# The second half of the residual moved ahead of the masked maxima in the last step of an attention tile

## The reference, cut to what matters

```
x = L0_attn_x                                   # 16 x 2048 x 1024, float32
# layernorm, attention with a window of 128, 16 heads of 64, residual
x = x + _L0_attn_ref(_layernorm(x), w_qkv, w_out)
# layernorm, then two linear layers with ternary weights and 8-bit activations,
# gelu between them, residual
x = x + _L0_ffn_ref(_layernorm(x), W1, b1, W2, b2)

allowed = (j <= i) & (j > i - WINDOW)
scores = jnp.where(allowed, scores, -jnp.inf)
attn = jax.nn.softmax(scores, axis=-1)
```

## Time and profile before

| what | us |
|---|---|
| median of 3 runs | 1665.79 |
| lowest and highest of these | 1577.72, 1676.39 |
| the profiled execution, device time | 1573.67 |
| its span on the slowest core (core 2) | 1571.9 |
| its spans on the eight cores | 1557.0 to 1571.9 |

### The profile page before, as it was taken

One profiled execution on the slowest core, in us unless ns is written; L12 is line 12 of the kernel. 1 busy time (PEld: TensorE's weight loads), 2 busy tenths in 40 slices (PEclk: granted clock), 3 DMA queues, 4 the chain that ended last, 5 costly groups with the idle time before them and its releaser, 6 DMA issues.

```text
span 1571.9 us, 33942 instructions; the slowest of 8 cores (1557.0 to 1571.9 us)
## 1 busy us (share of the span) xinstructions
PE 1489.5 (95%) x11685; PEld 838.6 (53%) x11748; DVE 1072.7 (68%) x2697; ACT 797.8 (51%) x1836; POOL 250.2 (16%) x199
## 2 busy tenths in 40 slices
PE   3789999999899999989999999999999999999998
PEld 3556677667566676644444444444444444444443
DVE  2468888888788999776666666666566666656653
ACT  3667877777677777754333333333333333333321
POOL 0000012222223333103010101101010110101000
PEclk9799999999999999999999999999999999999999
DMA  9768878677776676444424334343443424334332
GB/s 296 212 157 230 236 215 235 202 225 216 179 201 166 189 197 191 107 113 99 113 61 89 93 77 105 63 111 69 82 101 74 108 61 102 80 80 101 73 76 54
DMA packets 275113, 213.74 MB, mean 136 GB/s; under 512 B 237184, under 2 KB 237312, under 8 KB 274944
## 3 DMA queue, kind: packets, MB, share of 16 engines
q1 hardware_dynamic: 270336, 194.79, 49.3%
q0 software_dynamic: 4608, 16.78, 2.8%
HBM read 120.29 MB, written 33.55 MB: 98 GB/s over the span
## 4 chain that ended last, share of the span: by engine, by line
PE 76%; DVE 12%; issue 6%; DMA 2%; SPq 2%; ACT 1%; POOL 0%; DVEq 0%; ACTq 0%; POOLq 0%
PE f L204 30%; PE av L204 29%; PE sc L204 15%; DVE msc L473 4%; DVE xr L240 2%; SPq L190 2%; DVE lnc L331 1%; DMA wst<-wqkv 1%; DMA xlnT<-xln 1%; DVE PT L253 1%; DVE tern L227 1%; PE tA L209 1%; ACT probs L220 1%; PE tB L209 1%; POOL xln L227 0%
## 5 line engine op out<-in xcount | busy, mean ns | idle before, releaser
L204 PE MATMUL av<-W2q,hqT 128*128 128x512 fp8e4 x2048 | 447.2, 379 | 1.7 <-DVE msc L237 1.7
L220 ACT ACTIVATE hbuf<-hb 128x512 f32<-128x512 f32 x256 | 160.3, 629 | 450.5 <-DVE hb L237 450.4
L204 PEld LDWEIGHTS av<-W2q,hqT 128*128 128x128 bf16 x2048 | 200.0, 98 | 243.9 <-issue 2.2
L220 ACT ACTIVATE probs<-msc,cells 128x256 bf16<-128x256 f32 (+1 forms) x512 | 250.8, 491 | 95.7 <-DVE cells L473 95.0
L204 PE MATMUL f<-xlnT,wqkv_sb 128*128 128x128 bf16 x4096 | 258.1, 223 | 20.6 <-DMA xlnT<-xln 8.4
L204 PEld LDWEIGHTS f<-xlnT,wqkv_sb 128*128 128x128 bf16 x4096 | 239.8, 100 | 35.4 <-issue 35.2
L204 PE MATMUL f<-W1q,xlnT 128*128 128x512 fp8e4 x1040 | 235.6, 379 | 0.3 <-DVE hb L237 0.3
L204 PE MATMUL sc<-W1q,xlnT 128*128 128x512 fp8e4 x1008 | 227.8, 379 | 0.0
L473 DVE CUSTOM_DVE_ANT_0 msc<-sc,masks 128x256 f32<-128x256 f32 (+1 forms) x512 | 182.3, 411 | 45.7 <-PE sc L204 41.4
L220 ACT ACTIVATE hq<-hbuf,konst,fhc 128x1024 f16<-128x1024 f32 x128 | 148.3, 1229 | 88.6 <-DVE fhc L225 85.2
L204 PEld LDWEIGHTS f<-W1q,xlnT 128*128 128x128 bf16 x1040 | 101.6, 98 | 122.3 <-issue 0.9
(11 more groups left out here) (87 smaller groups left out, 1390.6 us busy)
## 6 DMA issues: line engine op xcount, KB each, us to landing
stg<-w1t SPq DMA_DIRECT2D x64, 512.0 KB, 7.5
stg<-w2t SPq DMA_DIRECT2D x64, 512.0 KB, 5.3
xr<-xc SPq DMA_DIRECT2D x32, 512.0 KB, 4.9
x1sp<-xr POOLq DMA_DIRECT2D x32, 512.0 KB, 6.3
xr<-x1sp SPq DMA_DIRECT2D x32, 512.0 KB, 4.6
y<-msc SPq DMA_DIRECT2D x31, 512.0 KB, 3.3
wst<-wqkv SPq DMA_DIRECT2D x24, 512.0 KB, 18.7
wst<-wout SPq DMA_DIRECT2D x8, 512.0 KB, 19.8
```

The lines of the kernel that those rows point to most:

```text
L204: return op("pe", lambda e: e.matmul(out=out, lhsT=lhsT, rhs=rhs, start=start, stop=stop), waits, sig)
L220: return op("act", lambda e: e.activation(out=out, in_=in_, func=func, **kw), waits)
```

## The change

In the last step of a tile (`c = 3`) `prev_ev()` is called after the score matmuls of the next step and before their masked maxima. In all other steps the order stays.

```diff
@@ -980,6 +980,10 @@
                 loads()
             if nxt:
                 s_pe(j + 1)
+            if c == 3 and prev_ev is not None:
+                prev_ev()
+                prev_ev = None
+            if nxt:
                 ttr(j + 1)
             if prev_ev is not None:
                 prev_ev()
```

## The result

| kernel | median us | ratio to before, fast executions | 95% interval |
|---|---|---|---|
| before (7 runs beside the change) | 1577.72 | | |
| the change (7 runs) | 1594.85 | 1.0121 | 1.0092 to 1.0151 |

The change makes the kernel 1.2% slower, about 19 us, by less than the 2% line and clearly outside its noise. The forecast was 1572.4 us with a range of 1563.5 to 1585, so it was wrong in sign and in size.

The account below looks back on a forecast made before the run. PE was taken as the bound, idle 37.2 us in attention. Of 10.1 us of residual waits, Q's transpose left 0.4 + 0.9 = 1.3 us to win: 1573.67 - 1.3 = 1572.4 us, range 1563.5 to 1585.

Parts of the forecast that it names:

- The stretch that decides: Attention: PE is busy 522.8 of 560 us, so at most 37.2 us can be won; FFN keeps its length.
- The wait for the residual: Ahead of step 0's scores, PE's 23 waits under `rsum`, 11.4 us, all vanish: 10.1 us less there.
- Two waits in series that end together: Behind the scores, Q still waits for its transpose's landing, so only 1.3 us is saved.
- The later masked maxima at no cost: On DVE the maxima come up to 0.77 us later, with 0.6 us of cover at the tightest: cost 0.
- rival D: Later maxima make PE wait at the scores in five late tiles: 2.5 us lost, 1576 us, chance 0.05.
- The spill's price: Spill stores go out up to 1.4 us earlier, nearer to or onto the transpose: taken as 0 us per tile.
- The bound above: Upper price of the earlier spill: 44 us of all spills on the DMA engines by 32 spills, 1.4 us each.
- Rival C: Earlier spill delays transpose landings, paid in full through Q: 5.8 to 40 us, 1578 to 1612 us, chance 0.15.

Follow-up runs that it names:

- All three edits together: The change, the transpose's chain ahead of norm(t, 0) and the spill held until the transpose landed, against the kernel before: ratio 0.9904, median 1556.63 us.

## Why the prediction was wrong

**The stretch that decides, right.** PE's idle time in attention is where everything happened.

**The wait for the residual, right.** It vanished: 11.4 us to none in the view of waits, 9.1 to -0.4 us in the balance. Scores to scores at step 3 is 4.56 us in nearly all tiles.

**Two waits in series that end together, right.** Q starts 0.25 us behind the landing in the changed kernel too. With the spill at its old time the ratio is 1.0004 (forecast: 0.9992). All three edits together bring 1.0%, more than the held spill with the change and the early transpose alone (0.3% each), as two waits in series would have it.

**The later masked maxima at no cost, right.** The run with the spill at its old time has them as late and loses nothing that can be seen. In one late tile of core 4 PE did wait 0.4 us for `cells` at the scores, which was rival D, in that tile only.

**The spill's price, wrong, and this is the step that failed.** The text took 0 us per tile as "the value of nearly all tiles". Measured, a transpose that the spill met was mostly 1.5 to 2.2 us late, and the landings grew by 26.9 us a core. The tiles that gave the 0 were all of one kind: there the spill is issued 1.4 us or more behind the transpose, and what the text read as an overlap that costs nothing was none. In the tile of the earlier trace rows not one packet of the spill ran before the landing. Both numbers that say this no longer holds were at hand: the spill comes up to 1.4 us earlier where no `tern` stands ahead, and it used to go out 1.5 us behind the transpose (311.61 and 310.13 in the earlier trace rows). Their difference is next to nothing. I followed one common tile, which has a `tern`, and never laid out the other kind, which makes up 11 of 28. In the tile of the earlier trace rows, called the nearest row, the first packet of the spill ran 2.6 us behind the transpose's issue, and the transpose's own packets were through 0.2 us later; it measured a brush at most, not a meeting, and an `instruction` packet ran in it as well. The transposes hit took 4.6 to 5.6 us.

**The bound above, a little low.** 1.4 us per tile was worked out from the share of the DMA engines that all spills take. A transpose that was met lost 1.5 us or more. In the tile at 156.30 the stores' time on the engines (1.5 us) is the delay; others lost up to 1 us more, so the engine time is near the price but doesn't bound it. As a total the ceiling of 40 us held, since not all tiles were hit.

**The chances.** Rival C, with its mechanism, its payment nearly in full through Q (23 of 27 us) and its sign, is what happened; it measured 23 us in the balance, between the two prices given (14.5 and 40 us), and 19 us in the time. It stood at 0.15, and the range ended at 0.4 us per tile. With the two kinds of tiles laid out the sum would have been, at the forecast's own upper price, 11 tiles by 1.4 us, 15 us slower, which is already beyond the range; at the prices measured since, 1.5 to 2.2 us, it is 17 to 24 us. The rule cited of the page "DMA: Bandwidth & Descriptors" of the Trainium skill, section "Queues, rings and completion order", that a DMA engine takes turns between queues packet by packet, pointed the right way. The changed kernel's landings (4.6 us and more) and those with the spill from ACT's queue (3.8 to 4.1) agree with it in that a spill in another queue delays the transpose. The turns themselves no run here shows: in the tile at 156.30 the transpose's packets ran mostly behind the stores'.

## What to carry to other kernels

An instruction that is moved takes along the DMAs that wait for it. Put the new issue time of each beside every transfer that the bound engine waits for, once for each kind of tile and not for a typical one. Before counting a wait as a gain, look what PE meets right behind it; if a second wait ends at the same moment, the two have to be shortened together (0.3% each, 1.0% together here). A DMA that has a long time to land can be held behind a critical one with one added semaphore wait, but that wait also holds what stands behind it in the issuing engine's queue: look where that goes.

## What the runs showed of the hardware

- A transposing DMA of a 128x1024 bf16 tile lands after 3.0 to 3.1 us. With 512 KB of stores issued from GpSimd within 0.2 us of it, it took 4.6 to 5.6 us (core 4); with 256 KB so, about 3.7 or 4.1, by core; with 512 KB issued 0.4 us ahead of it from ACT, 3.8 to 4.1; with 512 KB issued 0.9 us behind it, 3.0 to 3.7 in 13 of 17; 1.4 us behind, 3.0 to 3.3 in 26 of 27.
- Undisturbed, its 256-byte packets run from 1.2 to 2.6 us behind SP's issue. Stores issued from GpSimd can begin 1.2 us behind their issue (in the tile at 156.36) and can begin later: the spill issued at 311.61 in the kernel before had no packet by 313.18.
- A transpose during which an `instruction` packet (8 or 16 KB) ran on a DMA engine landed after more than 3.6 us in 434 of 698 cases, any other without a spill beside it in 20 of 1527.
- Loads of 512 KB that SP issued 1.3 us behind the transpose, in its own queue, were there in all kernels and left it at 3.0 to 3.1 us.
- A wait that a DMA ends can stand in the view under the name of an engine that was long done (13.7 of the 19.7 us under `probs` in the changed kernel); the landing of the transpose plus 0.25 us told it apart.
